# Two small weight loads issued by ScalarE, and a reordered tail of the last feed-forward

## The reference

```
h = jax.nn.silu(bitlinear158(x, w1, b1))
h = jax.nn.gelu(h, approximate=False)
h = layer_norm(h, ln_g, ln_b)
return bitlinear158(h, w2, b2)
```

## Time and profile before

| | |
|---|---|
| time, median of 3 executions | 550.28 us (548.55 to 550.74) |
| the profiled execution | 551.81 us, its span 549.9 us |
| mean granted TensorE clock | 0.957 |
| PE busy | 486.0 us (88%) |
| DVE busy | 447.5 us (81%) |
| ACT busy | 368.7 us (67%) |
| POOL busy | 273.4 us (50%) |

### The profile page before, as it was taken

One profiled execution on the slowest core, in us unless ns is written; L12 is line 12 of the kernel. 1 busy time (PEld: TensorE's weight loads), 2 busy tenths in 40 slices (PEclk: granted clock), 3 DMA queues, 4 the chain that ended last, 5 costly groups with the idle time before them and its releaser, 6 DMA issues.

```text
span 549.9 us, 10711 instructions
## 1 busy us (share of the span) xinstructions
PE 486.0 (88%) x3396; PEld 398.9 (73%) x3402; DVE 447.5 (81%) x1213; ACT 368.7 (67%) x864; POOL 273.4 (50%) x255
## 2 busy tenths in 40 slices
PE   8968888799998999998999999987999889997925
PEld 5454565466887667767889998976899779996804
DVE  4899999999867487985669568969789789776887
ACT  2787778594464557886756666687467886688644
POOL 1139999893107555302783587336782343333121
PEclk9959999999998999998999999999899999999867
DMA  6666887571887996925120035000351000000000
GB/s 163 169 167 187 225 272 235 176 219 48 227 272 221 283 310 211 307 82 179 50 76 2 22 71 64 2 1 18 61 86 13 1 1 2 21 2 1 1 20 19
DMA packets 52557, 61.65 MB, mean 112 GB/s; under 512 B 6284, under 2 KB 42742, under 8 KB 52502
## 3 DMA queue, kind: packets, MB, share of 16 engines
q1 hardware_dynamic: 48662, 49.43, 30.5%
q0 software_dynamic: 3840, 11.54, 8.9%
HBM read 54.27 MB, written 6.69 MB: 111 GB/s over the span
## 4 chain that ended last, share of the span: by engine, by line
PE 36%; issue 21%; DVE 20%; POOL 10%; ACT 9%; DMA 3%; DVEq 0%; SPq 0%; POOLq 0%; ACTq 0%
PE ps L1701 6%; PE ps L1640 4%; PE ps L1642 4%; PE ps L1641 4%; DVE hst L1957 4%; PE ps L1690 3%; DMA G<-token_rows,idx_x 2%; POOL dbu L635 2%; PE ps L1360 2%; PE ps L1558 2%; POOL pn L720 2%; POOL G L704 2%; POOL G L682 2%; DVE hc L1969 2%; PE ps L1368 1%
## 5 line engine op out<-in xcount | busy, mean ns | idle before, releaser
L720 POOL TENSOR_TENSOR pn<-pr,pinv 128x512 f32<-128x512 f32 x64 | 67.7, 1060 | 89.4 <-DVE pinv L2364 88.8
L635 POOL TENSOR_TENSOR dbu<-du,brow 128x512 f32<-128x512 f32 x64 | 82.4, 1321 | 22.3 <-DVE du L1944 18.7
L1084 ACT ACTIVATE pr<-ebuf,smin 128x256 f32<-128x256 f32 x128 | 63.7, 502 | 13.2 <-DVE smin L2355 6.8
L1701 PE MATMUL ps<-pT,cS 128*128 128x256 f32 x256 | 67.2, 385 | 0.0
L872 ACT ACTIVATE ps<-dtv,amat 128x510 f32<-128x510 f32 x64 | 44.0, 696 | 24.4 <-DVE hst L1957 19.5
L682 POOL DMA_INDIRECT G<-token_rows,idx_x x32 | 37.8, 1180 | 44.9 <-DVE wkv L2093 20.8
L704 POOL DMA_INDIRECT G<-expert_out,idx_g x48 | 51.1, 1066 | 11.5 <-issue 10.3
L1640 PE MATMUL ps<-xnT,mqk 128*128 128x256 f32 x128 | 47.1, 368 | 6.5 <-DVE qT L2325 3.3
L2355 DVE CUSTOM_DVE_ANT_0 ebuf<-ps,mbias 128x256 f32<-128x256 f32 x128 | 48.9, 419 | 4.6 <-issue 4.6
L1098 ACT ACTIVATE oT<-ps 128x256 fp32r<-128x256 f32 x64 | 24.4, 382 | 34.5 <-PE ps L1701 30.8
L1701 PEld LDWEIGHTS ps<-pT,cS 128*128 128x128 f32 x256 | 44.7, 193 | 3.9
(11 more groups left out here) (386 smaller groups left out, 1466.3 us busy)
## 6 DMA issues: line engine op xcount, KB each, us to landing
brow<-state_rows SPq DMA_DIRECT2D x16, 512.0 KB, 3.8
wdn<-in_L_ffn_wd SPq DMA_DIRECT2D x12, 384.0 KB, 5.2
ebuf<-state_rows SPq DMA_DIRECT2D x17, 256.0 KB, 5.3
wgu<-in_L_ffn_wg SPq DMA_DIRECT2D x11, 384.0 KB
wgu<-in_L_ffn_wu SPq DMA_DIRECT2D x11, 384.0 KB
expert_out<-xn SPq DMA_DIRECT2D x11, 256.0 KB
wo<-in_L_xattn_Wo SPq DMA_DIRECT2D x4, 512.0 KB, 5.9
wq<-in_L_xattn_Wq SPq DMA_DIRECT2D x4, 512.0 KB, 5.6
```

The source lines that it names most:

```text
L635: nc.gpsimd.tensor_tensor(dbu[:, j, :], du[:, j % 2, at:at + 512], brow[:, pair % BRING, j // 2, :], ALU.mult).then_inc(pool_dbu, 1)
L720: nc.gpsimd.tensor_tensor(pn[:, h % 2], pr[:, h % 2], pinv[:, h % 2, :].unsqueeze(2).to_broadcast([P, 2, L]), ALU.mult)\
L1084: last = A(pr[:, h % 2, tt, :], sneg[:, h % 2, tt, :], ACT.Exp, scale=-1.0, bias=smin[:, h % 2, tt:tt + 1], accum_out=psum_[:, h % 2, tt:t ...
L1701: last = pe.matmul(ps[:, 3 + 2 * (h % 2), 0:L], cS[:, b % 2, st, :], pT[:, h % 2, st, :], start=(st == 0), stop=(st == 1))
```

## The change

The two loads leave SP's list and stand at the top of ACT's list, `convw` first. In the tail, tile 0's `silu` becomes one ACT pass in place, so that `tail_gated` and `tail_tanh` are left for tile 1 alone. The dummy activation at slot 64 is now `Silu`, and a second one, `Gelu`, stands behind `tail_silu(1)`. ACT does tile 1's `tanh` before tile 0's deviation. `tail_middle` is one instruction, and on DVE `tail_middle(1)` stands ahead of `tail_normal(0)`. The wait of `rest_rows` is not touched by the diff: its count 7 is now reached by the first `tail_gated` of tile 1.

```diff
             dma(ctx_tm[:], t["ctx_1024"]...).then_inc(d_ctx, 16)
-                dma(win[:], t["L0_xattn_in_proj_w"].rearrange("(t p) d -> p t d", p=P)).then_inc(d_win, 16)
-                dma(convw[:], t["L0_xattn_conv_w"].rearrange("(t p) a k -> p t (a k)", p=P)).then_inc(d_win, 16)
                 dma(x[:], t["x"].rearrange("b (c p) h -> p (b c) h", p=P)).then_inc(d_x, 16)
...
             A = nc.scalar.activation
+                act.dma_start(convw[:], t["L0_xattn_conv_w"]...).then_inc(d_win, 16)
+                act.dma_start(win[:], t["L0_xattn_in_proj_w"]...).then_inc(d_win, 16)
             act.wait_ge(pool_steps, 2)
             A(spare_table[:, 0:1], ones[:, 0:1], ACT.Silu)
...
-            def tail_tanh(k, n):
-                act.wait_ge(f_h, 2 * B - 2 + 2 * k + n + 1)
+            def tail_silu(n):
+                act.wait_ge(f_h, 2 * B - 2 + n + 1)
+                part = hbuf[:, 0, 512 * n:512 * n + 512]
+                A(part, part, ACT.Silu).then_inc(f_silu, 1)
+            def tail_tanh(n):
+                act.wait_ge(f_h, 2 * B + n + 1)
...
             def tail_gelu(k, n):
-                act.wait_ge(f_gated, 2 * B - 2 + 2 * k + n + 1)
-                A(part, part, ACT.Gelu, scale=0.5, accum_out=fhalf[:, k, n:n + 1]).then_inc(f_act, 1)
+                if k == 0:
+                    act.wait_ge(f_silu, 2 * B - 2 + n + 1)
+                    A(part, part, ACT.Gelu, accum_out=fhalf[:, 0, n:n + 1]).then_inc(f_act, 1)
+                else:
+                    act.wait_ge(f_gated, 2 * B - 2 + n + 1)
+                    A(part, part, ACT.Gelu, scale=0.5, accum_out=fhalf[:, 1, n:n + 1]).then_inc(f_act, 1)
...
-                    preload(1, ACT.Gelu)
+                    preload(1, ACT.Silu)
...
             tail_turned(0)
-            tail_tanh(0, 0)
-            tail_tanh(0, 1)
+            tail_silu(0)
+            tail_silu(1)
+            preload(0, ACT.Gelu)
             tail_turned(1)
             tail_gelu(0, 0)
             tail_gelu(0, 1)
+            tail_tanh(0)
+            tail_tanh(1)
             tail_deviation(0)
-            tail_tanh(1, 0)
-            tail_tanh(1, 1)
             tail_gelu(1, 0)
             tail_gelu(1, 1)
...
             def tail_middle(k):
-                step(V.tensor_tensor(fsum[:, k:k + 1], fhalf[:, k, 0:1], fhalf[:, k, 1:2], ALU.add))
-                sync()
-                V.tensor_scalar(fmean[:, k:k + 1], fsum[:, k:k + 1], -1.0 / FI, None, ALU.mult).then_inc(f_mean, 1)
+                V.tensor_scalar(fmean[:, k:k + 1], fhalf[:, k, 0:1], fhalf[:, k, 1:2], -1.0 / FI, ALU.add, ALU.mult)\
+                    .then_inc(f_mean, 1)
...
             tail_round(1)
-            tail_gated(0, 0)
-            tail_gated(0, 1)
             finish(B - 2)
             tail_hidden(1, 0)
             tail_hidden(1, 1)
             tail_middle(0)
             tail_centred(0)
-            tail_gated(1, 0)
-            tail_gated(1, 1)
+            tail_gated(0)
+            tail_gated(1)
             tail_variance(0)
+            tail_middle(1)
             tail_normal(0)
-            tail_middle(1)
             tail_centred(1)
```

More of the change, by code:

```diff
@@ L810, in _ @@
             A = nc.scalar.activation
+            with nc.allow_non_contiguous_dma(reason="a few hundred values"):
+                act.dma_start(convw[:], t["L0_xattn_conv_w"].rearrange("(t p) a k -> p t (a k)", p=P)).then_inc(d_win, 16)
+                act.dma_start(win[:], t["L0_xattn_in_proj_w"].rearrange("(t p) d -> p t d", p=P)).then_inc(d_win, 16)
             act.wait_ge(pool_steps, 2)
@@ L1141, in tail_turned @@
                 A(xqT[:, H * k:H * k + H], bank(k).bitcast(BF16)[:, 0:H], ACT.Copy).then_inc(f_qT, 1)
-            def tail_tanh(k, n):
-                act.wait_ge(f_h, 2 * B - 2 + 2 * k + n + 1)
+            def tail_silu(n):
[4 more added lines that the diff above has]
+                act.wait_ge(f_h, 2 * B + n + 1)
                 act.wait_ge(f_act, 6 * B - 6)
-                A(tanhs[k][:, 512 * n:512 * n + 512], hbuf[:, k, 512 * n:512 * n + 512], ACT.Tanh, scale=0.5)\
+                A(tanhs[1][:, 512 * n:512 * n + 512], hbuf[:, 1, 512 * n:512 * n + 512], ACT.Tanh, scale=0.5)\
                     .then_inc(f_silu, 1)
             def tail_gelu(k, n):
-                act.wait_ge(f_gated, 2 * B - 2 + 2 * k + n + 1)
                 part = hbuf[:, k, 512 * n:512 * n + 512]
-                A(part, part, ACT.Gelu, scale=0.5, accum_out=fhalf[:, k, n:n + 1]).then_inc(f_act, 1)
+                if k == 0:
[4 more added lines that the diff above has]
+                    A(part, part, ACT.Gelu, scale=0.5, accum_out=fhalf[:, 1, n:n + 1]).then_inc(f_act, 1)
             def tail_deviation(k):
@@ L2592, in tail_hidden, with tail_gated @@
                                        ALU.mult, ALU.add).then_inc(f_h, 1)
[L2594 to L2598, removed]
+            def tail_gated(n):
+                dve.wait_ge(f_silu, 2 * B + n + 1)
+                part = hbuf[:, 1, 512 * n:512 * n + 512]
+                V.scalar_tensor_tensor(part, tanhs[1][:, 512 * n:512 * n + 512], 1.0, part, ALU.add, ALU.mult)\
                     .then_inc(f_gated, 1)
@@ L2603, in tail_middle @@
                 dve.wait_ge(f_act, 6 * B - 6 + 3 * k + 2)
-                step, sync = tail_steps(1)
-                step(V.tensor_tensor(fsum[:, k:k + 1], fhalf[:, k, 0:1], fhalf[:, k, 1:2], ALU.add))
-                sync()
-                V.tensor_scalar(fmean[:, k:k + 1], fsum[:, k:k + 1], -1.0 / FI, None, ALU.mult).then_inc(f_mean, 1)
+                V.tensor_scalar(fmean[:, k:k + 1], fhalf[:, k, 0:1], fhalf[:, k, 1:2], -1.0 / FI, ALU.add, ALU.mult)\
+                    .then_inc(f_mean, 1)
             def tail_variance(k):
```

## The result

| | before | changed |
|---|---|---|
| median of 20 runs each | 550.01 us (548.02 to 552.53) | 552.40 us (550.01 to 558.57) |
| profiled execution, its span | 551.81, 549.9 us | 553.68, 551.9 us |
| mean granted clock | 0.957 | 0.959 |

The ratio is 1.004, 95% interval 1.0026 to 1.0055, which is 1.4 to 3.0 us. The ratio leaves out one slow execution of the changed kernel (558.57). By the medians the change makes the kernel 2.4 us slower. I had forecast 0.55 us faster, and the measured median lies 0.8 us above my range.

The account below looks back on a forecast made before the run. No single engine was taken to bound the kernel, but the work ending last at head and tail. Head -0.65 (-1.1 + 0.45) and tail +0.1 gave -0.55 us, from a median of 550.28 to 549.7; range 547.7 to 551.6.

Parts of the forecast that it names:

- The step that failed: Head: `win` lands at 5.6, then the context is late, so the gain is at most 1.1 us.
- My bound of +0.9 for the head: Head, worst case: the context is late by 2.0 us, all that `win` and `convw` take behind it.
- My rival of a late context: Head: the context becomes the late load, delayed by over 1.1 us; head +0.9, total 551.3 us; chance 0.14.
- where I took 0.45: Head: delay of the context from sharing the DMA engines with `win`, 128 KB at 299 GB/s; 0.45 us.
- The 0.8 and 1.3 for ACT's issues and their being first: Start of ACT's list: `convw` issued at 0.8, `win` at 1.3, ahead of the table load; rival's chance 0.08.
- The tail, +0.1: Tail: the reordered steps put centring of tile 1 at 536.42 against 536.33, 0.1 us later.
- the 1.65 us that I took from the earlier trace: Tail, POOL: duration of `rest_rows` beside DVE's second gate, against 1.28 to 1.29 at its other places.
- where I had bound it at -0.65: Tail, lower bound: if `rest_rows` cost nothing, centring of tile 1 would come 0.65 us sooner.
- The rival with both halves paying in full: Head and tail: free DMA share takes the loads, `rest_rows` runs beside the gates; -1.1 - 0.65, 548.5 us; chance 0.15.
- A term that rested on one sample: Head: `convw` issued 1.1 us sooner, its old 4.76 us kept, so a gain of up to 1.1 us.
- The bound from the context: Head: context transposes and ACT's copies let L1284 start at about 7.15 instead of 8.28, capping the gain at 1.1 us.
- My sign that I am wrong: Middle of the kernel: the forecast is wrong if the time between 13 and 518 us changes by more than 1 us.

Follow-up runs that it names:

- the loads alone: Only the two loads move to ACT's queue, `convw` then `win`, tail as in the kernel before: 552.38 us against 550.01, ratio 1.0034.
- with PE busy: Kernel before with both loads moved to ACT and ten more dummy matmuls ahead of PE's wait for `win`: 552.39 us against 549.60, ratio 1.0037.
- with `x` later: Kernel before with both loads moved to ACT and `x` issued behind five small loads on SP: 550.08 us against 549.60, ratio 1.0005.
- with eight dummies: Kernel before with eight instead of ten warm-up dummy matmuls on PE ahead of the context's transposes: 550.05 us against 550.76, ratio 0.9979.

## Why the prediction was wrong

**The step that failed** is in the head: "So 1.1 us is the most that the head can give, whatever time the two loads take below 5.6." I put `win` down as "issued at 1.3, as before", and let it land in time. I asked whether `x` might come late by the move, and whether anybody gains from its coming earlier ("this earns nothing"), but not what its coming earlier costs others. `x` moved from behind both weights to beside `win`. Measured: `win` lands 7.70, 6.51, 7.06 and 6.96 us after its issue in four traces of this arrangement (the changed kernel, the loads alone, with PE busy, the changed kernel again), against 3.7 to 4.1 in the six traces that show it where SP issues it ahead of `x`. Two experiments show the cause: with `win` first on ACT it lands in 3.9 us and `convw`, now beside `x`, in 6.3; with `x` later `win` lands in 4.95, and the time can't be told from before. My bound of +0.9 for the head was set by what `win` and `convw` take, 2.0 us for 132 KB; the load that mattered, 1024 KB, stood in none of my terms.

The Trainium skill, DMA: Bandwidth & Descriptors, section "Queues, rings and completion order", says that a DMA engine serves the queues that have work in turn, a packet of one and then a packet of the other. As an estimate from it: once the context has landed at 5.2, 128 KB of `win` and as much of `x`, or twice as much if its packets are twice as large, would take 0.8 to 1.2 us at 337 GB/s, and `win` would land at 6.0 to 6.4. The trace does not agree, with 8.99, and neither do the other three, with 7.80, 8.36 and 8.26. There `win` lands 0.6 to 1.3 us ahead of `x`, in the first one 0.2, and no run here shows why it comes so late.

**The second term that I did not have** is PE's clock. PE waits 2.6 us for `win`, its granted clock falls to 0.50, and `wink` to tap grows by 1.3 us, from 2.49. In the loads alone and in the second execution PE waits only 1.2 us, the clock falls a little later, and the growth is 1.15 and 0.55 (8.28 to 11.32). With PE kept busy it does not fall and nothing grows. It follows from the first failure.

**Steps that held.** My rival of a late context is out: the context lands 4.4 us after its issue instead of 3.9, and 4.1 in the three other traces, so 0.5 or 0.2 late where I took 0.45. That PE's transposes begin 0.34 later, near my number, is luck in part: PE goes to them straight from its dummies, which last 4.24 us there and 3.98 before. In the other three they begin 0.56 to 0.62 later, behind dummies of 4.5 to 4.6 us, with the context there since 4.9. The 0.8 and 1.3 for ACT's issues and their being first: 0.78 and 1.29. The tail, +0.1: the trace of the changed tail alone shows +0.05 at the same centring, its median +0.2 with an interval from -0.6 to +1.2. `rest_rows` holds POOL for the 1.65 us that I took from the earlier trace rows, starts just behind the first gate, and the root follows it; without it the centring is 0.74 sooner than with it, 0.69 sooner than before, where I had bound it at -0.65. The rival with both halves paying in full needed this, and so fell.

**A term that rested on one sample.** I counted 1.1 us of gain from the 4.76 us of `convw`. In four traces with the loads of before, `wink` begins at 6.69, 6.50, 6.05 and 5.55, and at 7.26 in a fifth, with eight dummies. In the one with 5.55, the changed tail alone, the chain of waits holds no load: it goes from PE's dummies (1.19, for 4.44 us) straight to the context's transposes, and there is nothing to gain:

```profile
1.19 4.44 PE ps L1278 x20
```

The bound from the context was the right idea, but I did not see PE's share in it: `convw` on ACT alone, with `win` ahead of `x`, brings the weights at 5.3 and times as before.

**From 3.6 us to 2.4.** In the changed kernel's trace the tap is 3.6 us late; the mean over its trace, the loads alone and its second execution (12.80, 11.47, 11.32) is 11.86, against 8.91 over four traces with the loads of before (9.18, 8.99, 8.70, 8.77): 2.95 us. Timed are 2.4 by the medians for the change and for the loads alone, 2.2 and 1.9 by the ratios. The rest is smaller than the spread of the experts' stage: from first gather to first `pn` it is 96.5 and 94.2 us in two executions of the kernel before, 94.8 and 96.7 in two of the changed one. So that 4.20 us at 166 shrink to 2.48 behind the experts in this pair of traces is chance. My sign that I am wrong "if the time between 13 and 518 us changes by more than 1 us" came true and was badly chosen: from the statistics to the tail's first `x` it went from 506.8 to 504.7, which is the spread of that stage and says nothing of the change.

## What to carry to other kernels

A DMA that leaves a queue moves all that stood behind it forward. Price those too, above all a large one that now runs beside the small one on which the chain waits: here 1024 KB moved by 1.1 us held 128 KB back by 2.4 to 4.0 us.

A wait for a load in one trace is one sample. Before counting on it, ask which engine would be late next, and look for it in a second execution: here the second limit, PE's own warm-up, left 1.0 us to gain in one execution of `convw` alone on ACT (tap at 8.17 for 9.18) and nothing in the other (9.46).

A gain in one trace can be PE's clock. Before crediting 0.6 us to a reordering, look at the granted clock of the step where it arises, in two executions.

## What was unexpected of the hardware

- A 4 KB load (convw), second on ACT's queue and issued together with `x`, took 6.3 us; first on that queue and issued with the context it took 3.4 to 3.9.
- The same ten dummy matmuls of fp32 took 4.6 us in one execution and 3.9 in the next of the same kernel, and the eight transposes behind them 1.76 and 1.05. The profile's clock reads 1.00 in both, yet a piece takes 421 ns early on, as at a granted 0.50 later, and 272 after that. What ends the early stretch was not found.
- The table load for ScalarE's `Gelu` behind `Silu` in the tail took 1.28 us (527.90), so the two are not in one table; it was hidden but for 0.2 us.
